# A selective scan on one Trainium2 core: the second and third scan of a step become one scan of 1,024 columns

## What is computed

```python
xc = depthwise_conv1d(xm, taps=3); xm = silu(xc + c1_b)
dt_r, Bm, Cm = split(xm @ xp_w.T, [6, 16, 16])
dt = softplus(dt_r @ dt_w.T + dt_b)
A = -exp(A_log)                          # [96, 16]
def step(h, (dt_t, x_t, B_t, C_t)):      # one position
    da = exp(dt_t[:, None] * A)
    h = da * h + (dt_t * x_t)[:, None] * B_t[None, :]
    y = (h * C_t).sum(n)
y = (ys + xm * Dp) * silu(z)
```

## Time and profile before

| | us |
|---|---|
| median of 3 runs | 1552.34 |
| lowest, highest | 1547.71, 1555.3 |
| the profiled execution | 1553.88 |
| its span | 1552.1 |
| DVE busy in the span | 1204.2 (78%) |
| ACT busy | 1105.8 (71%) |
| PE busy | 1157.5 (75%) |
| POOL busy | 947.4 (61%) |

### The profile page before, as it was taken

One profiled execution on the slowest core, in us unless ns is written; L12 is line 12 of the kernel. 1 busy time (PEld: TensorE's weight loads), 2 busy tenths in 40 slices (PEclk: granted clock), 3 DMA queues, 4 the chain that ended last, 5 costly groups with the idle time before them and its releaser, 6 DMA issues. The chain is left out here.

```text
span 1552.1 us, 14783 instructions
## 1 busy us (share of the span) xinstructions
PE 1157.5 (75%) x3828; PEld 419.5 (27%) x3828; DVE 1204.2 (78%) x1198; ACT 1105.8 (71%) x1643; POOL 947.4 (61%) x501
## 2 busy tenths in 40 slices
PE   4899625655653777777888888888888888656995
PEld 2343201111111555532222222222222222003563
DVE  1666538998982777612999999999999999991775
ACT  2687257776751777748999999999999999731564
POOL 2500049999994333315989888888988888940000
PEclk8999855555555999978999999999999998556997
DMA  5455450300003233318887778887777787706572
GB/s 144 127 144 133 106 166 30 108 1 27 28 14 102 72 102 88 91 50 189 196 190 186 180 182 184 183 194 186 181 180 184 185 183 176 156 23 132 137 169 56
DMA packets 137487, 200.56 MB, mean 129 GB/s; under 512 B 27099, under 2 KB 69130, under 8 KB 136916
## 3 DMA queue, kind: packets, MB, share of 16 engines
q1 hardware_dynamic: 133964, 193.27, 50.8%
q0 software_dynamic: 1280, 3.74, 0.8%
q10 hardware_dynamic: 2160, 2.61, 0.7%
HBM read 145.93 MB, written 53.63 MB: 129 GB/s over the span
## 5 line engine op out<-in xcount | busy, mean ns | idle before, releaser
L1803 DVE TENSOR_TENSOR_SCAN m_h<-m_qa,m_state,m_ub 128x512 f32<-128x512 f32 x384 | 464.9, 1270 | 55.5 <-POOL m_ub L1389 52.4
L1389 POOL TENSOR_TENSOR m_ub<-m_dlb,m_bt 128x1536 f32<-128x1536 f32 x128 | 440.3, 3441 | 20.7 <-DMA m_dlb<-scratch_dldu 10.2
L1754 ACT ACTIVATE m_qa<-m_dlb,k_a 128x512 f32<-128x512 f32 x384 | 253.7, 684 | 77.6 <-DVE m_h L1803 66.2
L1814 DVE TENSOR_TENSOR m_g<-m_h,m_qc 128x1536 f32<-128x1536 f32 x128 | 222.0, 1735 | 1.0 <-issue 0.8
L1635 PE MATMUL m_qy<-m_g,k_seld 128*32 128x512 f32 x768 | 161.4, 711 | 0.0
L1110 POOL TENSOR_TENSOR b_u<-b_dl,b_z 128x1024 f32<-128x1024 f32 x48 | 125.2, 2609 | 17.7 <-ACT b_dl L1000 15.9
L1618 PE MATMUL m_qc<-m_cp,k_selc 112*128 112x512 bf16 x128 | 53.2, 416 | 110.0 <-DVE m_g L1814 109.5
L1121 POOL TENSOR_TENSOR b_y<-b_y,b_g 128x1024 f32<-128x1024 f32 x48 | 130.8, 2724 | 3.4 <-DVE b_g L1073 3.2
L966 PE MATMUL b_qb<-b_bc,k_pack_sel 96*128 96x512 bf16 x96 | 58.9, 614 | 94.8 <-DVE b_u L1051 94.7
L1550 PE MATMUL m_qf<-m_cva,k_conv 113*96 113x504 f32 (+1 forms) x192 | 117.2, 759 | 8.5 <-PEq L1141 5.0
L1051 DVE TENSOR_TENSOR b_u<-b_u,b_qb 128x512 f32<-128x512 f32 x96 | 65.4, 681 | 43.0 <-PE b_qb L966 29.5
(11 more groups left out here) (191 smaller groups left out, 2346.3 us busy)
## 6 DMA issues: line engine op xcount, KB each, us to landing
m_dlb<-scratch_dldu SPq DMA_DIRECT2D x128, 384.0 KB, 9.7
m_bt<-scratch_brow SPq DMA_DIRECT2D x128, 256.0 KB, 5.6
scratch_dldu<-m_dldu SPq DMA_DIRECT2D x32, 384.0 KB, 3.1
scratch_z<-a_z SPq DMA_DIRECT2D x24, 256.0 KB
scratch_y<-b_y SPq DMA_DIRECT2D x12, 512.0 KB, 2.6
c_y<-scratch_y SPq DMA_DIRECT2D x16, 384.0 KB, 3.4
scratch_gate<-m_gt SPq DMA_DIRECT2D x32, 192.0 KB, 2.6
scratch_y<-m_yo SPq DMA_DIRECT2D x32, 192.0 KB, 11.2
```

Source lines behind the costliest of these rows:

```text
L1389: nc.gpsimd.tensor_tensor(ub[k % 3][:], dlb[u % 2][:, J:2 * J, :], bcast(bt[u % 2][:, n, :], J), ALU.mult).then_inc(ub_ready, 1)
L1754: nc.scalar.activation(q_a[:, j, :], dlb[u % 2][:, j, :], ACT.Exp, scale=G["a1"][:, j, n:n + 1]).then_inc(da, 1)
L1803: nc.vector.tensor_tensor_scan(h[k % 3][:, j, :], q_a[:, j, :], ub[k % 3][:, j, :], state[:, k % NS, j:j + 1], ALU.mult, ALU.add).then_inc ...
L1814: nc.vector.tensor_tensor(g[k % 2][:], h[k % 3][:], bcast(q_c[:], J), ALU.mult).then_inc(read, 1)
```

## The change

VectorE's three scans of a step become two. The scan of j = 0 stays as it is. The scans of j = 1 and j = 2 become one instruction of 1,024 columns over both pieces, with the constant 0.0 as start value. So that the state of piece 1 does not run on into piece 2, and both start from their own carried state, three things are added:

- The decay at column 0 of the pieces 1 and 2 is zero. VectorE writes it once; the exponentials of these pieces then cover the columns 1 to 511.
- The carried state enters by the drive: once a unit GpSimd multiplies `dt` of the first column by A (`edges`, 128 x 8), ScalarE takes its exponential (`edge_decay`, 128 x 8), and GpSimd multiplies that by the carried states (`carry_of`, 128 x 8).
- Once a step GpSimd adds the result to the first column of the drive of pieces 1 and 2 (`join`, 128 x 2). It does so for step k + 1 after it has made the drive of step k + 2.

`ub_ready`, for which VectorE waits, is now raised by `join`; the drive itself raises the new `ub_made`. ScalarE's exponentials of the pieces 1 and 2 both wait for the joined scan of the step before. `rest_of` with its `alone` moves from s = 0 to s = 1.

```diff
@@ gpsimd
                 if k >= 3:
-                    pool.wait_ge(scanned, 3 * (k - 3) + 3)
+                    pool.wait_ge(scanned, 2 * (k - 3) + 2)
                 nc.gpsimd.tensor_tensor(ub[k % 3][:], dlb[u % 2][:, J:2 * J, :], bcast(bt[u % 2][:, n, :], J),
-                                        ALU.mult).then_inc(ub_ready, 1)
+                                        ALU.mult).then_inc(ub_made, 1)
+            def edges(u):
...
+                pool.wait_ge(dlb_loaded[u % 2], 64 * (u // 2 + 1))
...
+                    pool.wait_ge(carried, u)
+                nc.gpsimd.tensor_tensor(edge[:], bcast(dlb[u % 2][:, 1:J, 0], 4),
+                                        G["a1"][:, 1:J, :].rearrange("p j n -> p n j"), ALU.mult).then_inc(edged, 1)
+            def carry_of(u):
...
+                pool.wait_ge(edge_da, u + 1)
+                if u >= 4:
+                    pool.wait_ge(kept, 4 * (u - 4) + 4)
+                at = 4 * (u % B)
+                nc.gpsimd.tensor_tensor(carry[u % 2][:], edge[:], state[:, at:at + 4, 1:J], ALU.mult).then_inc(carried, 1)
+            def join(k):
...
+                pool.wait_ge(ub_made, k + 1)
+                pool.wait_ge(carried, u + 1)
+                first = ub[k % 3][:, 1:J, 0]
+                nc.gpsimd.tensor_tensor(first, first, carry[u % 2][:, n, :], ALU.add).then_inc(ub_ready, 1)
...
+                if s == 2:
+                    edges(t + 1)
                 drive(k + 2)
+                if s == 3:
+                    carry_of(t + 1)
+                join(k + 1)
                 if s == 2:
                     outputs(t - 1)
-                if s == 0:
+                if s == 1:
                     alone(k + 3, t + 2, t - 1)
                     rest_of(t + 2)
@@ scalar
                     if k >= 1:
-                        act.wait_ge(scanned, 3 * (k - 1) + j + 1)
-                    nc.scalar.activation(q_a[:, j, :], dlb[u % 2][:, j, :], ACT.Exp,
+                        act.wait_ge(scanned, 2 * (k - 1) + (1 if j == 0 else 2))
...
+                    nc.scalar.activation(q_a[:, j, at:CH], dlb[u % 2][:, j, at:CH], ACT.Exp,
...
+            def edge_decay(u):
...
+                act.wait_ge(edged, u + 1)
+                nc.scalar.activation(edge[:], edge[:], ACT.Exp).then_inc(edge_da, 1)
...
                 decay(k + 1)
                 keep(k)
+                if s == 2:
+                    edge_decay(t + 1)
@@ vector
-                for j in range(J):
-                    dve.wait_ge(da, 3 * k + j + 1)
-                    nc.vector.tensor_tensor_scan(h[k % 3][:, j, :], q_a[:, j, :], ub[k % 3][:, j, :],
-                                                 state[:, k % NS, j:j + 1], ALU.mult, ALU.add).then_inc(scanned, 1)
+                dve.wait_ge(da, 3 * k + 1)
+                nc.vector.tensor_tensor_scan(h[k % 3][:, 0, :], q_a[:, 0, :], ub[k % 3][:, 0, :],
+                                             state[:, k % NS, 0:1], ALU.mult, ALU.add).then_inc(scanned, 1)
+                dve.wait_ge(da, 3 * k + 3)
...
+                rows = (x[:, 1:J, :].rearrange("p j t -> p (j t)") for x in (h[k % 3], q_a, ub[k % 3]))
+                nc.vector.tensor_tensor_scan(*rows, 0.0, ALU.mult, ALU.add).then_inc(scanned, 1)
```

More of the change, by code:

```diff
@@ L1334, in mid1_phase @@
         state = m.sb("m_state", [P, NS, J])
+        edge = m.sb("m_edge", [P, 4, J - 1])
+        carry = [m.sb(f"m_carry{r}", [P, 4, J - 1]) for r in range(2)]
         q_a = m.ps("m_qa", [P, J, CH])
@@ L1340, in mid1_phase @@
          xa_ready, gt_ready, sz_ready, xm_ready, tail, u_out, bc_out, top_out, rest_out, middle_out, parted, da, kept,
-         du_ready, ub_ready, delta, scanned, read, y_out, y_ready) = (
+         du_ready, ub_ready, delta, scanned, read, y_out, y_ready, ub_made, edged, edge_da, carried, cleared) = (
             m.sem(f"m_{n}") for n in (
@@ L1344, in mid1_phase @@
                 "xa_ready", "gt_ready", "sz_ready", "xm_ready", "tail", "u_out", "bc_out", "top_out", "rest_out", "middle_out", "parted", "da", "kept",
-                "du_ready", "ub_ready", "delta", "scanned", "read", "y_out", "y_ready"))
+                "du_ready", "ub_ready", "delta", "scanned", "read", "y_out", "y_ready", "ub_made", "edged", "edge_da", "carried", "cleared"))
         cv_loaded, gt_stored, dldu_stored, dlb_loaded, bt_loaded, y_stored = (
@@ L1387, in drive @@
                 if k >= 3:
-                    pool.wait_ge(scanned, 3 * (k - 3) + 3)
+                    pool.wait_ge(scanned, 2 * (k - 3) + 2)
                 nc.gpsimd.tensor_tensor(ub[k % 3][:], dlb[u % 2][:, J:2 * J, :], bcast(bt[u % 2][:, n, :], J),
-                                        ALU.mult).then_inc(ub_ready, 1)
+                                        ALU.mult).then_inc(ub_made, 1)
+            def edges(u):
+                if not exists(u):
+                    return
+                pool.wait_ge(dlb_loaded[u % 2], 64 * (u // 2 + 1))
+                if u >= 1:
+                    pool.wait_ge(carried, u)
+                nc.gpsimd.tensor_tensor(edge[:], bcast(dlb[u % 2][:, 1:J, 0], 4),
+                                        G["a1"][:, 1:J, :].rearrange("p j n -> p n j"), ALU.mult).then_inc(edged, 1)
+            def carry_of(u):
+                if not exists(u):
+                    return
+                pool.wait_ge(edge_da, u + 1)
[4 more added lines that the diff above has]
+            def join(k):
+                if not steps(k):
+                    return
+                u, n = divmod(k, 4)
+                pool.wait_ge(ub_made, k + 1)
+                pool.wait_ge(carried, u + 1)
+                first = ub[k % 3][:, 1:J, 0]
+                nc.gpsimd.tensor_tensor(first, first, carry[u % 2][:, n, :], ALU.add).then_inc(ub_ready, 1)
             lo, mid, top = (slice(at, at + NS) for at in C_PARTS)
@@ L1399, in alone @@
                 if drives > 0:
-                    pool.wait_ge(ub_ready, min(drives, 4 * UNITS))
+                    pool.wait_ge(ub_made, min(drives, 4 * UNITS))
+                if drives > 1:
+                    pool.wait_ge(ub_ready, min(drives - 1, 4 * UNITS))
                 pool.wait_ge(du_ready, products)
@@ L1752, in decay @@
                     if k >= 1:
-                        act.wait_ge(scanned, 3 * (k - 1) + j + 1)
-                    nc.scalar.activation(q_a[:, j, :], dlb[u % 2][:, j, :], ACT.Exp,
-                                         scale=G["a1"][:, j, n:n + 1]).then_inc(da, 1)
+                        act.wait_ge(scanned, 2 * (k - 1) + (1 if j == 0 else 2))
+                    elif j == 1:
+                        act.wait_ge(cleared, 1)
+                    at = 0 if j == 0 else 1
+                    nc.scalar.activation(q_a[:, j, at:CH], dlb[u % 2][:, j, at:CH], ACT.Exp,
+                                         scale=G["a1"][:, j, n:n + 1]).then_inc(da, 1)
+            def edge_decay(u):
+                if not exists(u):
+                    return
+                act.wait_ge(edged, u + 1)
+                nc.scalar.activation(edge[:], edge[:], ACT.Exp).then_inc(edge_da, 1)
             def y_evict(v):
@@ L1768, in keep @@
                     return
-                act.wait_ge(scanned, 3 * k + 3)
+                act.wait_ge(scanned, 2 * k + 2)
+                if k >= NS:
+                    act.wait_ge(carried, (k - NS) // 4 + 5)
                 nc.scalar.activation(state[:, k % NS, :], h[k % 3][:, :, CH - 1], ACT.Identity).then_inc(kept, 1)
@@ L1790, in _ @@
         def _(dve):
+            nc.vector.memset(q_a[:, 1:J, 0], 0.0).then_inc(cleared, 1)
             dve.wait_ge(zeroed, NZ)
@@ L1800, in scans @@
                     dve.wait_ge(kept, k - 2)
-                for j in range(J):
-                    dve.wait_ge(da, 3 * k + j + 1)
-                    nc.vector.tensor_tensor_scan(h[k % 3][:, j, :], q_a[:, j, :], ub[k % 3][:, j, :],
-                                                 state[:, k % NS, j:j + 1], ALU.mult, ALU.add).then_inc(scanned, 1)
+                dve.wait_ge(da, 3 * k + 1)
+                nc.vector.tensor_tensor_scan(h[k % 3][:, 0, :], q_a[:, 0, :], ub[k % 3][:, 0, :],
+                                             state[:, k % NS, 0:1], ALU.mult, ALU.add).then_inc(scanned, 1)
+                dve.wait_ge(da, 3 * k + 3)
+                if k == 0:
+                    dve.wait_ge(cleared, 1)
+                rows = (x[:, 1:J, :].rearrange("p j t -> p (j t)") for x in (h[k % 3], q_a, ub[k % 3]))
+                nc.vector.tensor_tensor_scan(*rows, 0.0, ALU.mult, ALU.add).then_inc(scanned, 1)
             def times_c(k):
@@ L1808, in times_c @@
                     return
-                dve.wait_ge(scanned, 3 * k + 3)
+                dve.wait_ge(scanned, 2 * k + 2)
                 dve.wait_ge(c_mm, k + 1)
```

## The result

| | before | after |
|---|---|---|
| median of 20 runs, us | 1550.26 | 1555.78 |
| lowest, highest | 1544.95, 1555.3 | 1548.53, 1566.76 |
| profiled execution, span | 1553.88, 1552.1 | 1556.77, 1555.0 |

The ratio is 1.0040, with a 95% interval of 1.0025 to 1.0055: some 6 us slower (0.4%). The prediction said 0.46% slower. Its 1559.5 us stood on the three runs that were known then (median 1552.34); over 20 runs the kernel before has 1550.26, so 2.1 of the 3.7 us between 1559.5 and 1555.78 are that.

The account below looks back on a forecast made before the run. A loop of VectorE, which sets the pace, and nearly full ScalarE. Start +5.3, shorter steps -20.2, window delay +21.9, unit 0 +0.4, last scans -0.2: +7.2 us, median 1552.34 to 1559.5, range 1549 to 1572.

Parts of the forecast that it names:

- A step: VectorE's own step in the loop: 5.03 us for 5.19, 0.16 less, over 126 steps -20.2 us.
- the rival with 5.09 us a step: Joined scan 61 ns dearer, like one with start value from memory: 1565.5 us, slower; chance 0.08.
- the saving of 0.075 us: Skill's rule for one VectorE instruction less: 0.075 us a step, about 10 us in all, giving 1567 us.
- The window: ScalarE's four SiLUs between two table loads: VectorE's scan behind them loses 1.01 us for 0.20, +21.9 us in 27 units.
- T: End of the scans of step 4t + 1, from which ScalarE works without a pause.
- ScalarE as the cause: Two exponentials, not one, wait when step 4t + 1's scans end; all ScalarE work behind them moves by 0.61 us.
- The first rival: ScalarE absorbs the second exponential and VectorE stays the bound: 1537 us, without any delay 1532; chance 0.11.
- GpSimd: Six new small instructions a unit at 0.29 us, 1.7 us; 20.4 of 21.13 us, all covered in the loop.
- The rival: GpSimd becomes the pace from 0.40 us for a small instruction with its wait; at 0.5, 1582 us; chance 0.10.
- The start: Start of the phase, behind GpSimd's first instructions: first scan 4.0 us later, second step 5.3 us later.
- `rest_of`: On GpSimd, one step later: ends its wait for ScalarE's copy, 2.23 us of room more in a unit.
- The sum: From start of step 1 to the end: +5.3, -20.2, +21.9, +0.4, -0.2, that is +7.2 us.

Follow-up runs that it names:

- the kernel with two orders: Changed kernel, but in step 4t + 1 alone pieces 0 and 1 are joined and piece 2 is scanned last; 1540.62 us, ratio 0.9931.
- the kernel with both edits: Changed kernel with pieces 0 and 1 joined in step 4t+1 and ScalarE's copy of y at the end of s = 0; 1531.6 us.
- the two edits that shorten its chain: Changed kernel with pieces 0 and 1 joined in step 4t+1 alone: 1540.62 us; changed kernel with copy of y at end of s=0: 1542.76 us.
- the edit that lengthens it: Changed kernel with all three pieces in one scan of 1,536 columns; 1645.27 us, ratio 1.0605.

## Why the prediction was right

Its forecast came true by its own mechanism.

- **A step.** Predicted 5.03 us, measured 5.02. The first layer's scan of the same shape gave the number (2.284 us, here 2.267); the rival with 5.09 us a step is out, and so is the saving of 0.075 us that the Trainium skill ("Vector Engine (DVE) Microarchitecture Reference", Measured stream behaviour on trn2) would give for one instruction less: measured are 0.17. But the prediction has the parts of this saving wrong. It puts 61 ns down to the start value and leaves the rest to the joining; the change takes away two start values that are read from memory. With such a start value a scan of 512 columns takes 1.19 us from start to start (1016.55 to 1017.74), with a constant one 1.12 (1002.64 to 1003.76 in the kernel with two orders). Three separate scans, two of them with a constant, would by these rows take 1.19 + 2 x 1.12 = 3.43 us, an estimate; before it was 3.54, joined it is 3.37. So some 0.11 us go with the start values and some 0.06 with the instruction, less than the 0.075; the scan of all three pieces, one instruction less again, saved 0.03. A kernel that brings the carried states in by the drive but leaves the scans separate would keep ScalarE's order of before and lose only those 0.06 us a step; no run tried it. That the whole saving is there when nothing waits is shown by the kernel with both edits: 20.10 us for four steps.
- **The window.** The scan behind it was predicted at T + 7.56; it stands at 1022.55 - 1014.99 = 7.56. The delay against VectorE alone (1019.92 + 1.65 = 1021.57) is 0.98 us, predicted 0.97 and another 0.04 for the last exponential. Those 0.04 us did not come: the joined scan follows its first scan by 1.20 us, as without a wait (1.19). The unit is 21.07 (21.13 predicted).
- **ScalarE as the cause.** Shown by the two edits that shorten its chain, alone (20.57 and 20.59) and together (20.10), and by the edit that lengthens it (one scan, 23.86). The first rival, that ScalarE absorbs the second exponential, spoke of its 1.7 us of rest in 21; that rest lies where ScalarE waits for a joined scan, 0.96 us ahead of T (the row at 1015.02) and most of what is left in the step after the window, and none of it lies between T and the late decays.
- **GpSimd.** The small instructions were put at 0.19 us and 0.1 between; they take 0.19 to 0.21, and in the unit from 1003.62 the six with what passes behind them come to 1.65 us (predicted 1.7), 0.28 apiece. They cost nothing in the loop, as the run without them shows. The rival needed 0.40 apiece.
- **The start.** Predicted 4.0 and 5.3 us later, measured 4.05 and 5.38; the run without carried states gives 4.3 to 5.1 us back.
- **`rest_of`.** Costed at nothing, and nothing by itself (1.000).
- **The sum.** Predicted +7.2 us. From GpSimd's first instruction to the end of the last scan the phase has grown by (1401.62 - 725.09) - (1393.21 - 722.88) = 6.2 us; that the unit is 0.06 us shorter than predicted makes 1.6 us less, and the four longer units, which nobody foresaw, 1.0 more, so the parts come to 6.6, within 0.5 us. That these two misses went against each other is luck, though of less than 2 us. The medians of 20 runs differ by 5.5 us. The two profiled executions differ by 2.9 only: work outside the phase, the same in both, was 3.3 us shorter after, 2.2 longer ahead of it and 5.5 shorter behind it. One profiled execution of each would have misled by half of the effect; the phase's own stretch and the medians do not.

## What to carry to other kernels

Before joining instructions on the busiest engine, look who is released by each of the parts: a part that ends early lets another engine start early, and joined they release it together, late. ScalarE was busy for 19.28 of 21 us here, and that number hides that its rest lies at the wrong place. Follow the released engine's rows from the release to the next thing waited for, and if they have no gap, weigh the joined instruction's gain against each row that moves. Take something off that chain first, or join different parts on the two sides of it, and the same edit turns from a small loss into a gain.

## Of the hardware, not expected

A scan with both inputs in SBUF stood still while GpSimd worked on SBUF (1.28 us became 4.06 in the mean), and a join of 0.19 us became 1.36 in the mean while scans ran. The multiplication by C, with one input in PSUM, kept its 1.72 us beside the same drives. The function-table load began only after `keep` ahead of it had ended (0.21 us behind the start of `keep`, which takes 0.19), which is why taking 0.57 us of work away from in front of it gave 0.48. And a start value read from memory costs a scan 0.07 to 0.08 us from start to start, more than the 0.03 to 0.06 of a further scan instruction.
